# GpSimd halves the eight expert outputs twice, two transposes a tile instead of four, and the residual added in the last column sweep

## The reference

```python
# x: (16, 64, 36, 100) float32, B C H W
def conv_ref(x, w_d, w_u, w_r, w_l):       # four sweeps, 9 taps, pad 4
    # over H: new = row + relu(conv1d(carry, w)), down with w_d, then up with w_u
    # over W: the same on columns, right with w_r, then left with w_l
    # the first and the last row (column) stay as they are in the backward sweep
    ...

def ffn_ref(x, router_w, router_b, expert_w, expert_b):   # 8 experts, 64 -> 64
    router_probs = softmax(x @ router_w + router_b, axis=-1)
    top_p, top_i = top_k(router_probs, 2)
    top_p = top_p / sum(top_p, axis=-1, keepdims=True)
    expert_out = einsum('bnd,edc->bnec', x, expert_w) + expert_b
    gathered = take_along_axis(expert_out, top_i[..., None], axis=2)
    return einsum('bnk,bnkc->bnc', top_p, gathered)

x = x + conv_ref(_ln_c(x), w_d, w_u, w_r, w_l)   # _ln_c: norm over the channels
t = _to_tokens(x)
t = t + ffn_ref(_ln_t(t), router_w, router_b, expert_w, expert_b)
x = _from_tokens(t, x)
```

## Time and profile before

| | us |
|---|---|
| median of 3 runs | 1489.31 |
| lowest, highest | 1487.41, 1489.89 |
| profiled execution, its own time | 1490.23 |
| its span, first to last instruction | 1488.4 |
| TensorE matmuls busy | 1417.2 |
| VectorE busy | 846.6 |
| ScalarE busy | 770.1 |
| GpSimd busy | 518.3 |

### The profile page before, as it was taken

How to read it: one execution, slowest core, us unless ns; L and a number is a source line. 1 busy time by engine, 2 the same in 40 slices (tenths; PEclk the granted TensorE clock), 3 DMA queues, 4 the chain that set the end, 5 groups by cost and what they waited for, 6 DMA issues and landing times.

```text
span 1488.4 us, 30314 instructions
## 1 busy us (share of the span) xinstructions
PE 1417.2 (95%) x9398; PEld 1202.8 (81%) x9398; DVE 846.6 (57%) x1751; ACT 770.1 (52%) x2349; POOL 518.3 (35%) x444
## 2 busy tenths in 40 slices
PE   7899999999998999999999998989999999989997
PEld 5899999999998999999999997555565556555654
DVE  4787888655553222222222222677777777777776
ACT  5567677434343222222222223666777677776774
POOL 2466666000000000000000002366667666676666
PEclk9999999999999999999999999799999999999999
DMA  4111111000000000000000001011211121111101
GB/s 138 45 50 60 66 47 63 23 0 0 0 0 0 0 0 0 0 0 0 0 0 0 0 0 36 9 45 45 88 44 44 44 76 56 44 44 53 58 23 45
DMA packets 17659, 46.41 MB, mean 31 GB/s; under 512 B 3168, under 2 KB 3168, under 8 KB 17632
## 3 DMA queue, kind: packets, MB, share of 16 engines
q1 hardware_dynamic: 17488, 45.76, 8.9%
q10 hardware_dynamic: 144, 0.33, 0.1%
HBM read 31.33 MB, written 14.75 MB: 31 GB/s over the span
## 4 chain that ended last, share of the span: by engine, by line
PE 81%; ACT 7%; DVE 6%; issue 4%; DMA 0%; DVEq 0%; POOL 0%; POOLq 0%; ACTq 0%
PE twin L922 31%; PE twin L839 25%; PE twin L980 9%; PE twin L992 4%; PE twin L962 4%; PE twin L949 3%; ACT scratch L460 2%; PE twin L830 2%; PE twin L940 2%; PE twin L824 2%; DVE scratch L761 1%; DVE parts L701 1%; ACT late L460 1%; ACT lnv L436 1%; ACT rstd L438 1%
## 5 line engine op out<-in xcount | busy, mean ns | idle before, releaser
L922 PE MATMUL twin<-kbuf,late 128*128 128x136 f32 (+2 forms) x3940 | 457.2, 279 | 5.0 <-DVE kbuf L671 5.0
L922 PEld LDWEIGHTS twin<-kbuf,late 128*128 128x128 f32 x3940 | 457.0, 191 | 5.3 <-DVE kbuf L671 5.3
L839 PE MATMUL twin<-parts 128*128 128x384 f32 (+2 forms) x2070 | 394.8, 343 | 0.0
L839 PEld LDWEIGHTS twin<-parts 128*128 128x128 f32 x2070 | 373.1, 189 | 2.9 <-issue 2.5
L677 DVE SCALAR_TENSOR_TENSOR kbuf<-twin,act_buf 128x144 f32<-128x144 f32 x394 | 121.2, 308 | 336.4 <-PE twin L922 336.4
L282 POOL TENSOR_TENSOR act_buf<-act_buf,x_in 128x400 f32 (+1 forms) x72 | 74.4, 1038 | 660.4 <-ACT act_buf L418 660.4
L418 ACT ACTIVATE act_buf<-kbuf 128x144 f32 x394 | 127.1, 323 | 331.3 <-DVE kbuf L677 331.3
L980 PE MATMUL twin<-em,parts 64*128 64x512 f32 x1404 | 227.6, 429 | 4.4 <-ACT scratch L460 2.2
L289 POOL TENSOR_TENSOR scratch<-scratch 128x512 f32<-128x512 f32 x126 | 160.8, 1280 | 103.2 <-DVE scratch L761 53.2
L980 PEld LDWEIGHTS twin<-em,parts 64*128 64x128 f32 x1404 | 115.0, 186 | 57.3 <-issue 31.0
L761 DVE TENSOR_TENSOR scratch<-twin,scratch 128x512 f32<-128x512 f32 (+1 forms) x126 | 114.9, 912 | 29.5 <-PE twin L980 29.5
(11 more groups left out here) (100 smaller groups left out, 1520.3 us busy)
## 6 DMA issues: line engine op xcount, KB each, us to landing
x_in<-x SPq DMA_DIRECT2D x72, 400.0 KB, 3.7
result<-act_buf SPq DMA_DIRECT2D x36, 400.0 KB, 2.9
scratch<-L_conv_w_d ACTq DMA_DIRECT2D x1, 320.0 KB, 4.9
scratch<-L_conv_w_u SPq DMA_DIRECT2D x1, 320.0 KB, 6.5
late<-L_conv_w_r SPq DMA_DIRECT2D x1, 320.0 KB, 6.5
late<-L_conv_w_l SPq DMA_DIRECT2D x1, 320.0 KB, 7.1
ew<-L_ffn_expert_w SPq DMA_DIRECT2D x2, 128.0 KB, 6.2
eb<-L_ffn_expert_b SPq DMA_DIRECT2D x1, 256.0 KB, 4.6
```

Of the source, the lines that this page charges most:

```text
L839: last = mm(acc[:, lo:hi], vw[:, k, wpart, si], carry[:, cpart, g, lo + s * BG:hi + s * BG], start=first and si == 0, stop=final and si == ...
L922: last = mm(banks[CONV[g]][:, lo * BG:hi * BG], hw[:, k, si], kbuf[:, g, lo + s:hi + s].rearrange("p j b -> p (j b)"), start=si == 0, stop ...
```

## The change

In the token stage GpSimd adds twice: experts 4 to 7 onto 0 to 3 as before, and then, after a wait for its own first add, 2 and 3 onto 0 and 1 (256 elements a partition). `sum_experts` makes two transposes for each tile instead of four and waits for the second add.

The residual leaves the token stage. In the left-going column sweep GpSimd takes over the copy from `kbuf` into `cols` from ScalarE and adds `x` in it: two adds of 144 elements a step. Column 0, which that sweep leaves as it is, gets its residual in two adds at the end. `x` is laid out a second time in DRAM, by columns (`x_col`), and SyncE loads it in 20 blocks of five columns into the two slots of `x_in`. TensorE waits once, before the token stage, for all columns. GpSimd's regions have nothing but tiles left, and SyncE only stores in the token stage.

```diff
+        COLS = 5
+        NBLK = W // COLS
+        x_blk = x_in[:, :, :, :].rearrange("p s c n -> p s (c n)")[:, :, 0:COLS * REG * HP // W].rearrange(
+            "p s (i g j b) -> p s i g j b", i=COLS, g=G, j=HP)
...
+            def load_columns(k, slot):
+                sp.dma_start(x_in[:, slot].rearrange("p c n -> p (c n)")[:, 0:COLS * REG * HP // W], x_col[k]).then_inc(s_xc[slot], 16)
+
             for slot in range(2):
                 sp.wait_ge(s_d, CH * (HP - 1 + slot))
-                load(slot, slot)
+                load_columns(slot, slot)
+            with sp.Fori(1, NBLK // 2) as i:
+                for slot in range(2):
+                    for g in range(G):
+                        sp.wait_ge(s_cb[g], W + 2 * COLS * (i - 1) + COLS * (slot + 1) - 1)
+                    load_columns(2 * i + slot, slot)
...
-            def residual(j, slot, c):
-                g, h = c // 2, c % 2
-                t = cols[:, j, g, h * WP:(h + 1) * WP].rearrange("p (w a) b -> p w a b", a=2)
-                src = x_in[:, slot, 2 * g:2 * g + 2].rearrange("p a (h w b) -> p h w a b", h=2, b=BG)[:, h]
-                nc.gpsimd.tensor_tensor(t, t, src, ALU.add).then_inc(s_t, 1)
+            def copy_back(u, i, slot, w):
+                for g in range(G):
+                    pool.wait_ge(s_k[g], u + 1)
+                    nc.gpsimd.tensor_tensor(cols[:, :, g, w], kbuf[:, g], x_blk[:, slot, i, g], ALU.add).then_inc(s_cb[g], 1)
+
+            def columns(k, slot, visit, count=COLS):
+
+                pool.wait_ge(s_xc[slot], 16 * visit)
+                for i in range(count):
+                    copy_back(k * COLS + (W - 1 + i), i, slot, k * -COLS + (W - 1 - i))
...
+            for g in range(G):
+                t = cols[:, :, g, 0]
+                nc.gpsimd.tensor_tensor(t, t, x_blk[:, 1, COLS - 1, g], ALU.add).then_inc(s_cb[g], 1)
...
                 nc.gpsimd.tensor_tensor(buf[:, 0:4], buf[:, 0:4], buf[:, 4:8], ALU.add).then_inc(s_ps, 1)
...
+                pool.wait_ge(s_ps, 2 * (TILES * j + p) + 1)
+                nc.gpsimd.tensor_tensor(buf[:, 0:2], buf[:, 0:2], buf[:, 2:4], ALU.add).then_inc(s_ps, 1)
...
-            with act.Fori(1, W) as u:
+            with act.Fori(1, W - 1) as u:
                 copy_back(u, u)
-            with act.Fori(W, 2 * W - 2) as u:
-                w = u * -1 + (2 * W - 2)
-                copy_back(u, w)
...
-                pe.wait_ge(s_t, n + 1)
...
-                pe.wait_ge(s_ps, n + 1)
+                pe.wait_ge(s_ps, 2 * (n + 1))
...
-                for e in range(E // 2):
+                for e in range(E // 4):
                     last = mm(banks[SUM][:, at:at + TN], stage(slot, p)[:, e], ident[:, :],
-                              start=e == 0, stop=e == E // 2 - 1, is_transpose=True)
+                              start=e == 0, stop=e == E // 4 - 1, is_transpose=True)
...
             pe.wait_ge(s_em, 10)
+            for g in range(G):
+                pe.wait_ge(s_cb[g], 2 * W - 1)
```

More of the change, by code:

```diff
@@ L10, with metaformer_kernel @@
 AX = mybir.AxisListType
-def metaformer_kernel(nc, x, w_d, w_u, w_r, w_l, router_w, router_b, expert_w, expert_b, out):
+def metaformer_kernel(nc, x, x_col, w_d, w_u, w_r, w_l, router_w, router_b, expert_w, expert_b, out):
     HP, P, G, W, BG = out.shape
@@ L173, in metaformer_kernel @@
         s_hm = [sem(f"s_hm{g}") for g in range(G)]
+        s_xc = [sem("s_xc0"), sem("s_xc1")]
         s_cb = [sem(f"s_cb{g}") for g in range(G)]
-        s_t = sem("s_t")
         s_d2 = sem("s_d2")
@@ L232, in store @@
                     sp.dma_start(out[j, :, g], cols[:, j, g]).then_inc(s_out, 16)
[L234 to L244, removed]
+            with sp.Fori(0, HP) as j:
                 store(j)
@@ L275, in _ @@
                         split_x(slot, c, CH * (2 * i + slot) + c, c % 2)
-            def residual(j, slot, c):
-                g, h = c // 2, c % 2
-                t = cols[:, j, g, h * WP:(h + 1) * WP].rearrange("p (w a) b -> p w a b", a=2)
-                src = x_in[:, slot, 2 * g:2 * g + 2].rearrange("p a (h w b) -> p h w a b", h=2, b=BG)[:, h]
-                nc.gpsimd.tensor_tensor(t, t, src, ALU.add).then_inc(s_t, 1)
+            def copy_back(u, i, slot, w):
[6 more added lines that the diff above has]
+                    copy_back(k * COLS + (W - 1 + i), i, slot, k * -COLS + (W - 1 - i))
+            for slot in range(2):
+                columns(slot, slot, 1)
+            with pool.Fori(1, NBLK // 2 - 1) as k:
+                for slot in range(2):
+                    columns(2 * k + slot, slot, k + 1)
+            columns(NBLK - 2, 0, NBLK // 2)
+            columns(NBLK - 1, 1, NBLK // 2, COLS - 1)
+            for g in range(G):
+                t = cols[:, :, g, 0]
+                nc.gpsimd.tensor_tensor(t, t, x_blk[:, 1, COLS - 1, g], ALU.add).then_inc(s_cb[g], 1)
             def pair_sums(j, slot, p):
@@ L289, in pair_sums, with region @@
                 nc.gpsimd.tensor_tensor(buf[:, 0:4], buf[:, 0:4], buf[:, 4:8], ALU.add).then_inc(s_ps, 1)
-            def region(j, slot, ahead, visit):
+                pool.wait_ge(s_ps, 2 * (TILES * j + p) + 1)
+                nc.gpsimd.tensor_tensor(buf[:, 0:2], buf[:, 0:2], buf[:, 2:4], ALU.add).then_inc(s_ps, 1)
+            def region(j, slot):
                 for p in range(TILES):
[L293 to L311, removed]
+                    pair_sums(j, slot, p)
+            with pool.Fori(0, HP // 2) as i:
+                region(2 * i, 0)
+                region(2 * i + 1, 1)
         @block.scalar
@@ L1038, in _ @@
                 sum_experts(HP - 1, 1, p)
-_INS = ['x', 'L0_conv_w_d', 'L0_conv_w_u', 'L0_conv_w_r', 'L0_conv_w_l',
+_INS = ['x', 'x_col', 'L0_conv_w_d', 'L0_conv_w_u', 'L0_conv_w_r', 'L0_conv_w_l',
         'L0_ffn_router_w', 'L0_ffn_router_b', 'L0_ffn_expert_w', 'L0_ffn_expert_b']
@@ L1050, in lay_rows, with lay_columns @@
     return np.ascontiguousarray(v).reshape(h // 2, 2 * c, GROUPS_OF_BATCH, -1)
+def lay_columns(np, x, cols=5):
+    b, c, h, w = x.shape
+    v = x[:, :, :, ::-1].reshape(GROUPS_OF_BATCH, b // GROUPS_OF_BATCH, c, h // 2, 2, w // cols, cols).transpose(5, 4, 2, 6, 0, 3, 1)
+    return np.ascontiguousarray(v).reshape(w // cols, 2 * c, -1)
 def lay_taps(np, w):
@@ L1082 @@
     for name in _INS:
-        a = np.ascontiguousarray(inputs[name])
+        a = np.ascontiguousarray(inputs['x' if name == 'x_col' else name])
         if name == 'x':
             a = lay_rows(np, a)
+        elif name == 'x_col':
+            a = lay_columns(np, a)
         elif 'conv' in name:
```

## The result

The changed kernel takes 1507.51 us (median of 4 runs, 1502.95 to 1512.7), the kernel before beside it 1488.46 us. The ratio is 1.013, with a 95% interval of 1.0112 to 1.0148: slower by 19 us. The profiled execution took 1508.46 us, its span is 1506.6.

What follows compares the result with a forecast made beforehand. A 19.66 us latency chain, then 16.04 us of gapless TensorE, set each token region. From 1490.23 us: 0 steady regions, +4.8 last region, -0.2 residual, +6.3 clock = 1501.1; the runs' median, 0.9 lower, gives 1500 us, range 1488 to 1510.

Steps and rivals of the forecast that it cites:

- The chain: Token stage, experts of tile 9 to GpSimd's start on next region's tile 2: 19.66 us of latency without a transpose.
- The second add: GpSimd's 256-element add: 0.73 us plus 0.08 wait, 2.05 us a tile, GpSimd busy 26.7 of 30.3 us.
- The new path: Second variance matmul to experts of tile 9, through GpSimd's tiles 2 to 6: 16.03 us against 16.04, regions stay 30.3.
- TensorE's own path: Second variance matmul to experts of tile 9 by TensorE alone: 13.5 us after eight pairs of transposes less, 2.5 us.
- rival 2: Cheap second add, 0.64 us or less, and quiet clock: 1486 us, at most 40 us less, 1454; chance 0.12.
- The last region: Last token region at GpSimd's pace: tiles 2 to 12 take 20.5 us against 16.20; together +4.8 us.
- The residual: Residual adds moved to the second column sweep: hidden, step stays 2.31 us; about -0.2 us before the first token matmul.
- The clock: TensorE idler ahead of the variance wait, so its clock falls in four more regions of 16 (none to eight): +6.3 us.
- The row that the prediction set against the rule: 4.70 us from 1480.70, TensorE doing only 1.97 us of transposes, clock at 1.00: transposes seem to count.

Runs made afterwards that it cites:

- The filler: Changed kernel plus six idle transposes of the identity behind the experts of tile 12: 1515.59 us, ratio 1.0203; added to second adds on five tiles: 1480.66 us.
- the run with five tiles: Changed kernel with the second add and two transposes only on tiles 0, 1, 3, 4 and 5, others one add, four transposes: 1484.04 us, ratio 0.9973.

## Why the prediction was right, step by step

**The chain.** Right: 19.59 us after, 19.66 before, with the two waits for VectorE in it. It is the reading in order of time that says this; by busy shares TensorE bounded the stage.

**The second add.** 0.73 us forecast, 0.731 measured; its wait 0.08, 0.08; 2.05 us a tile, 2.05. GpSimd is recorded busy 25.8 us of a region where 27 was said. The line through two lengths of the same instruction was good for both new lengths (0.48 forecast for 144 elements, 0.490 measured).

**The new path.** 16.03 us from the second variance matmul to the experts of tile 9 forecast, 1213.16 - 1197.10 = 16.06 measured, and a region at full clock 30.27 to 30.3. The runs with the second add on tiles 2 to 6 only (30.34) and off them (30.14) show it apart. Two terms were off. Two transposes cost 0.37 us from their start to the next experts, not 0.31. And a pair less gives 0.22 us, not the 0.31 that busy time gave, so eight pairs are worth 1.8 us and not 2.5: TensorE's own path, put at 13.5 us, was 14.9 in the run without the second add (1188.23 to 1203.16), with 0.4 of waits for ScalarE in it. A region paced by GpSimd shows neither, but the 40 us that rival 2 could gain at most were too many: 16 x (16.04 - 14.9) is 18.

**The last region.** +4.8 us forecast, +5.7 measured; GpSimd's part, 20.5 forecast, was 20.61, and three falls of the clock against one are in the rest.

**The residual.** Nothing, as forecast: 1.0007, sweep step 2.31 us. Its start was seen at 919.97 instead of 920.38, but that went into the first regions, where +0.4 us stands for the -0.2 forecast. The double add with the residual left in place (1553 us) shows what the prediction didn't say: the move is what keeps the second add from costing more than twice as much.

**The clock.** The direction was right and the size too small. Four regions more were forecast at 1.56 us, 6.3 us in all, out of a range up to eight; nine regions with falls against one is eight more, and 16 regions take 12.0 us more. This term is 5.7 of the 7.4 us that the sum (1501.1) lies under the profiled execution; the last region has 0.9 more, the way to the first full region 0.6.

That 12.0 comes so near to the upper end of the term, eight falls for 12.6 us, is luck, since it is made of other parts. A fall behind the variance wait costs about 1.0 us in a region of the changed kernel, not 1.56, and the eight of them make some 8 us; the three at tiles 5 to 8, which the prediction didn't see, make most of the rest, about 2 us each. The idle time that was to bring the eight was put too high as well: 2.2 us were forecast for the stretch from tile 9 to the variance matmul, and 0.31 + 0.20 + 1.30 = 1.8 stand ahead of the fall at 1222.4, where 1.6 stood before. The filler took all eight away, so that wait has a part in them.

The cause given, lost transposes, is half of it: with all four transposes and the second add the clock fell nine times, and with the transposes lost and no second add twelve times. By the Trainium skill (TensorE: Matmul & The Clock Gate, Part 4) transposes don't count as TensorE being busy in the same way, and losing them would have changed nothing; that doesn't agree with the twelve falls of the run that only loses them. The idle transposes at tiles 4 to 8 that didn't end the falls there go the rule's way, the idle matmuls that didn't either don't. The row that the prediction set against the rule is weak: it stops at 1485.40, and there the clock did fall, 1.0 us behind the last transpose.

```profile
1485.40:1488.40 3.00, 0.00 (x0) 0.00 (x0) 0.00 (x0) 0.00 (x0) 0.00 (x0) 0.50 0.68 273
```

What stays open is what tiles 5 to 8 lack. Two of the three falls of the changed kernel there follow a wait of 0.43 us for GpSimd by some 3 us, but four in the run without the second add follow no such wait, and the one of the run with five tiles came after 10.2 us in which TensorE was recorded busy for 10.16.

## What to carry to other kernels

An engine that is 93% busy can still have most of its loop set by a chain of latencies. Before work is moved from it to another engine, find in the order of time the stretch where it runs without a gap, and take work from it there only; with the double add on five tiles the kernel was 0.3% faster (0.5% with the filler), on all thirteen 1.3% slower. Price the receiving engine's path in the same stretch: here five adds of 0.8 us took back all that eight pairs of transposes had given. Here a TensorE with less work lost by its clock what it had gained, so what is gained in waits has to be checked for falls, region by region.

## What the runs showed of the hardware

Taking work from TensorE cost as much by the clock as it gave: twelve falls in 16 regions for a kernel that differs from the one with the residual moved alone only by 468 transposes less, which gave back all of 1.1 us a region. The clock also fell with TensorE recorded busy for 10.16 of the 10.2 us before, so a high busy share in the records doesn't tell that it is safe. Falls at one place of a loop that repeats can be regular (every second region with the second adds off the path), and emptying one place (8 to 0 with a filler) brought more of them at another (3 to 11). Work that is there only to keep TensorE busy, 0.9, 2.5 and 4.5 us of it a full-clock region by the records, didn't pay in any of the three runs that added it to the changed kernel (1516, 1529 and 1513 us against 1507.5; the last of these can't be told from it). GpSimd's fp32 add of two tensors costs 0.17 us and 2.16 ns an element from 144 to 512 elements, whatever the strides were here.
